# ACT issues the loads of the first modulation's weights on its own queue

## The chip, the cores and the metric

The kernel runs on one core of a Trainium2 chip. The metric is the device time of one execution in microseconds (us); shown are the median of several executions and one profiled execution with its trace.

## The reference, cut to what matters

Two transformer layers (a PixArt-like one with adaptive layer norm from a condition, then one with rotary embeddings) run over 32 sequences of 128 tokens with 256 channels, 16 heads of 16 channels, and 1024 hidden channels. The part at issue is the very first thing that layer 0 computes:

```python
mod = jax.nn.silu(t_emb) @ ada_w + ada_b        # t_emb (32, 256), ada_w (256, 1536)
shift_sa, scale_sa, gate_sa, shift_ff, scale_ff, gate_ff = jnp.split(mod, 6, axis=-1)
xm1 = _ln(x) * (1 + scale_sa) + shift_sa
qkv = (xm1 @ qkv_w + qkv_b).reshape(Bx, Nx, 3, H, HD)
```

Only `shift_sa` and `scale_sa`, the first 512 of the 1536 columns of `ada_w`, are needed before the first product with `qkv_w`. The rest of `ada_w` gives the gates and the modulation before the MLP.

## The kernel before, in words

The 32 sequences are worked through in 8 groups of 4, twice (once for each layer), and each group passes a fixed schedule of steps. One group's self-attention, cross-attention and MLP are laid over those of its neighbours. Five instruction streams (TensorE, ScalarE = ACT, VectorE = DVE, GpSimd = POOL, SyncE = SP) walk the same list of steps, `STEPS`, and meet at semaphores. Each stream's order is fixed by the code, so an instruction that waits holds back all that is behind it on its engine.

All transfers are issued by SP (lines 423 to 540), each with one `dma_start`, in this order: the condition `cond` (L427), four tiles of `x` (L429), seven small constants (L439), two transfers for the first 512 columns of `ada_w` (L441, 256 KB each, to `xs` and `side`, whose memory is free then), and then the weights of layer 0: `qkv_w` (768 KB, to `k_t`), `q_w` and `kv_w` (256 and 512 KB, to `probs_t`), the context (512 KB), `fc1_w` (1024 KB), the rest of `ada_w` (L530, 512 KB each), and more. None of these first issues waits for anything.

Every weight is split in two parts so that its products with rounded operands keep full precision. ACT makes the high part `w_hi` (L1049, a cast), DVE the low part `w_lo` (L1291, a subtraction). The first steps on each engine are:

- ACT: `Exp` of the condition (L1044, with its table load), wait for the constants, then `w_hi` of `qkv_w` when that has landed (`split_weights(0)`), then the modulation of the normalised tiles (`modulate`, L892, L897) once `mod_now` is there.
- DVE: it fills constants, makes `silu` from ACT's `Exp` (L1263 to L1267), prepares the biases once all seven constants have landed (L1270 on), takes the statistics of two tiles of `x`, makes `w_lo` of `qkv_w` (L1291, waits for `w_hi`), and only then adds the bias to the first modulation (L1281), adds one to the scales (L1286) and copies them to `mod_now` (L1170).
- TensorE: it waits for the constants, for `ada_loaded` and for `silu`, makes the first modulation (L833, 16 matmuls with `silu`, to `score`), transposes normalised tiles (L577), and multiplies with `w_hi` and `w_lo` (L546 to L548) for the first keys and queries (`p_unit`).

In the names of the trace `xs` and `side` are the two halves of `ada_w`, and `k_t<-in_L_xcond_qkv_w` is the load of `qkv_w`.

Of the kernel before, what the change touches and what calls it, by code (L numbers as in the profile page):

```python
# [16 lines left out]
P = 128  # L17
B, N, D, H = 32, 128, 256, 16
HD = D // H
DF = 4 * D  # L20
CT = D // P
# [162 lines left out]
def build_blocks(nc, a, x_mid, gates_dram, out):  # L184
    ctx = ExitStack()
    with ctx:
# [12 lines left out]
        def sem(name):  # L199
            return ctx.enter_context(nc.semaphore(name))  # L200
# [71 lines left out]
        def gate_ff(group):  # L272
# [11 lines left out]
        ada = [xs[:].rearrange("p a b c -> p (a b c)")[:, 0:6 * D],  # L284
               side[:].rearrange("p a b c -> p (a b c)")[:, 0:6 * D]]
# [24 lines left out]
        ada_loaded = sem("ada_loaded")  # L310
# [86 lines left out]
        def layer_of(group):  # L397
            return group // NG
# [26 lines left out]
        def _(sp):  # L425
            ada_w = a["L0_xcond_ada_w"].rearrange("(t p) n -> t p n", p=P)
# [3 lines left out]
            for dst, src in (  # L430
# [6 lines left out]
                (mask_cols_u8[:], a["mask_cols"]),  # L437
            ):
                sp.dma_start(dst, src).then_inc(c_loaded, 16)  # L439
            for c in range(CT):  # L440
                sp.dma_start(ada[c][:, 0:2 * D], ada_w[c, :, 0:2 * D]).then_inc(ada_loaded, 16)  # L441

            def load_weights(layer, c, to, signal):
                for name, col, kt, width in WEIGHTS[layer][c]:
# [428 lines left out]
        def _(act):  # L873
# [71 lines left out]
            def low_keys(group, unit):  # L945
                _, s, half = unit
                act.wait_ge(keys_summed, (group - NG) * 4 + 2 * s + half + 1)
                act.activation(k_t[s][:, :, 0, half * HALF:(half + 1) * HALF],
                               rot[:, 0, :].rearrange("p (t n) -> p t n", t=CT),
                               ACT.Identity, scale=head_mask[:, 0:1], bias=one_row[:, 0:1]).then_inc(keys_low, 1)  # L950
# [56 lines left out]
            def body():  # L1007
                for t in STEPS:
# [30 lines left out]
                    for group, step in live(t):  # L1039
                        if step - ACT_UNIT in UNIT_AT[layer_of(group)]:  # L1040
                            move_unit(group, UNITS.index(UNIT_AT[layer_of(group)][step - ACT_UNIT]))

            act.wait_ge(cond_loaded, 16)
            act.activation(silu_tmp[:], cond[:], ACT.Exp, scale=-1.0).then_inc(silu_step, 1)  # L1044
            act.wait_ge(c_loaded, 16 * CONST_LOADS)
# [10 lines left out]
        def _(dve):  # L1056
# [19 lines left out]
            def high_keys_out(group, n):  # L1076
                _, s, half = UNITS[n]
                dve.wait_ge(keys_low, group * 4 + 2 * s + half + 1)
                for t in range(CT):
                    op = dve.tensor_scalar(k_t[s][:, t, 1, half * HALF:(half + 1) * HALF],  # L1080
                                           p_unit[:, t * HALF:(t + 1) * HALF], head_mask[:, 1:2],
                                           key_bias[:, 1, 2 * s + t:2 * s + t + 1], ALU.mult, ALU.add)
                op.then_inc(keys_high, 1)
# [11 lines left out]
            def high_keys(group, unit):  # L1095
                _, s, half = unit
                dve.wait_ge(keys_summed, (group - NG) * 4 + 2 * s + half + 1)
                dve.tensor_scalar(k_t[s][:, :, 1, half * HALF:(half + 1) * HALF],
                                  rot[:, 0, :].rearrange("p (t n) -> p t n", t=CT),
                                  head_mask[:, 1:2], one_row[:, 1:2], ALU.mult, ALU.add).then_inc(keys_high, 1)  # L1100
# [391 lines left out]
```

## Time and profile before

| | |
|---|---|
| median of 3 executions | 1671.42 us (1670.57 to 1672.57) |
| profiled execution, its own time | 1671.03 us |
| its span, first to last instruction | 1669.2 us |
| TensorE matmul busy | 1501.2 us, 90% of the span |
| VectorE busy | 1096.9 us, 66% |
| ScalarE busy | 943.5 us, 57% |
| GpSimd busy | 719.1 us, 43% |
| mean granted TensorE clock | 0.972 |

The time lies 1.83 us above the span. Everything that the change touches happens in the first 20 us, before TensorE has its first large product.

### The profile page before, as it was taken

What the parts mean: (1) busy time and instruction counts of PE and PEld (TensorE: products, weight loads), DVE (VectorE), ACT (ScalarE), POOL (GpSimd) and SP (SyncE); (2) the same over time, 40 slices, a digit from 0 to 9 for tenths busy, and PEclk for the clock granted to TensorE, in tenths of its full rate; (3) what the DMA queues carried; (4) which work ended last, traced back from release to release, by engine and by line L of the source; (5) the groups of instructions that cost most, each with busy time, mean ns of one, the idle gap of its engine ahead of it and who ended that gap; (6) DMA issues with size and microseconds to landing.
All of it is one profiled execution on the core that took longest, in us unless ns stands there. A gap on an engine that the chain in (4) does not pass through costs nothing.

```text
span 1669.2 us, 44764 instructions
## 1 busy us (share of the span) xinstructions
PE 1501.2 (90%) x17760; PEld 1305.8 (78%) x17760; DVE 1096.9 (66%) x2373; ACT 943.5 (57%) x1722; POOL 719.1 (43%) x982
## 2 busy tenths in 40 slices
PE   4979999999999999999998989989899898989987
PEld 3868878787887878788786787878788787887866
DVE  4556766666766666667776766766767666676654
ACT  3456565556656565666645645556565555645543
POOL 3133424334242433335646445464554636455411
PEclk9899999999999999999998989999999999999988
DMA  6110100101010010100112000000000000000000
GB/s 211 47 47 10 45 16 15 52 13 55 10 46 15 15 53 13 55 27 27 33 45 65 11 17 15 14 27 11 17 15 14 26 12 17 18 24 2 2 14 14
DMA packets 34251, 49.39 MB, mean 30 GB/s; under 512 B 3488, under 2 KB 24928, under 8 KB 34048
## 3 DMA queue, kind: packets, MB, share of 16 engines
q1 hardware_dynamic: 34048, 46.54, 9.0%
q8 instruction: 145, 2.38, 0.6%
q14 instruction: 58, 0.48, 0.1%
HBM read 38.07 MB, written 8.45 MB: 28 GB/s over the span
## 4 chain that ended last, share of the span: by engine, by line
PE 67%; DVE 15%; issue 8%; ACT 8%; POOL 1%; DMA 0%; SPq 0%; DVEq 0%; ACTq 0%; POOLq 0%
PE score_t L670 8%; PE score L652 7%; PE p_unit L546 6%; PE p_unit L739 5%; PE p_mix L712 5%; PE p_unit L548 5%; PE p_unit L547 5%; DVE neg_max L1108 3%; PE p_out L548 3%; PE p_out L547 3%; PE p_out L546 3%; PE p_out L701 2%; PE p_mix L577 2%; PE score_t L546 2%; PE score_t L548 2%
## 5 line engine op out<-in xcount | busy, mean ns | idle before, releaser
L1108 DVE TENSOR_REDUCE neg_max<-score 128x8 f32<-128x1024 f32 x224 | 273.9, 1223 | 150.0 <-PE score L652 141.3
L652 PE MATMUL score<-k_t,q_t 32*128 32x256 f32 x1792 | 264.7, 413 | 54.1 <-DVE q_less L1118 28.7
L670 PE MATMUL score_t<-q_less,k_t 32*128 32x128 f32 x3584 | 273.4, 293 | 11.5 <-ACT probs_t L970 6.2
L670 PEld LDWEIGHTS score_t<-q_less,k_t 32*128 32x128 f32 x3584 | 229.8, 195 | 23.3 <-issue 14.9
L652 PEld LDWEIGHTS score<-k_t,q_t 32*128 32x128 f32 x1792 | 167.7, 194 | 94.8 <-issue 38.0
L972 ACT ACTIVATE probs_t<-score_t 128x1024 f32<-128x1024 f32 x168 | 172.0, 1024 | 113.4 <-PE score_t L670 100.7
L892 ACT ACTIVATE xt<-p_mix,mod_now 128x128 f32<-128x128 f32 x384 | 154.3, 454 | 94.3 <-PE p_mix L577 66.5
L1311 POOL TENSOR_TENSOR xt_lo<-xt,xt_hi 128x256 fp32r<-128x256 f32 x128 | 94.6, 739 | 243.1 <-ACT xt_hi L897 242.2
L739 PE MATMUL p_unit<-w_out,heads_t 128*128 128x256 f32 x512 | 144.9, 406 | 18.8 <-ACT q_t L936 8.2
L1156 DVE TENSOR_TENSOR hid_lo<-hid,hid_hi 128x256 fp32r<-128x256 f32 x256 | 145.2, 567 | 8.8
L546 PE MATMUL p_out<-w_hi,hid_lo 128*128 128x256 f32 x512 | 147.4, 288 | 0.8 <-issue 0.8
L1154 DVE CAST hid_hi<-hid 128x256 fp32r<-128x256 f32 x256 | 96.7, 378 | 73.5 <-ACT hid L957 73.4
L548 PE MATMUL p_out<-w_hi,hid_hi 128*128 128x256 f32 x512 | 144.5, 282 | 0.0
L547 PE MATMUL p_out<-w_lo,hid_hi 128*128 128x256 f32 x512 | 144.2, 282 | 0.0
L712 PE MATMUL p_mix<-probs_t,v_pad 128*32 128x128 f32 x4096 | 140.1, 278 | 0.0
L1118 DVE SCALAR_TENSOR_TENSOR q_less<-p_out,one_row,q_t 128x256 f32<-128x256 f32 x256 | 111.3, 477 | 33.8 <-PE p_out L701 33.8
L546 PE MATMUL p_unit<-xt_hi,w_lo 128*128 128x256 f32 x384 | 120.4, 314 | 11.7 <-DVE k_t L1080 7.7
L957 ACT ACTIVATE hid<-score_t,bias_cols 128x256 f32<-128x256 f32 x128 | 59.0, 475 | 117.6 <-PE score_t L548 106.6
L739 PEld LDWEIGHTS p_unit<-w_out,heads_t 128*128 128x128 f32 x512 | 87.2, 190 | 48.5 <-issue 27.3
L712 PEld LDWEIGHTS p_mix<-probs_t,v_pad 128*32 128x32 f32 x4096 | 105.2, 110 | 21.9 <-issue 21.7
L957 ACT ACTIVATE hid<-score,bias_cols 128x256 f32<-128x256 f32 x128 | 60.8, 475 | 99.7 <-PE score L548 55.6
L1304 POOL TENSOR_TENSOR rstd<-var_eps,minus_half 128x1 f32<-128x1 f32 x192 | 109.2, 569 | 15.0
(158 smaller groups left out, 4264.1 us busy)
## 6 DMA issues: line engine op xcount, KB each, us to landing
ctxt<-in_ctxT SPq DMA_DIRECT2D x16, 512.0 KB, 3.8
side<-gates SPq DMA_DIRECT2D x15, 512.0 KB, 5.5
x_new<-in_x SPq DMA_DIRECT2D x32, 128.0 KB, 2.0
x_mid<-xs SPq DMA_DIRECT2D x8, 512.0 KB, 3.4
x_new<-x_mid SPq DMA_DIRECT2D x32, 128.0 KB, 2.0
out<-xs SPq DMA_DIRECT2D x8, 512.0 KB, 2.9
k_t<-in_L_f_wT SPq DMA_DIRECT2D x2, 1024.0 KB, 5.7
probs_t<-in_L_xcond_fc_w SPq DMA_DIRECT2D x1, 1024.0 KB, 11.2
```

The lines of the kernel that those rows point to most:

```text
L546: pe.matmul(dst, lhs[1], rhs[0], start=first, stop=False, skip_group_check=shared)
L547: pe.matmul(dst, lhs[0], rhs[1], start=False, stop=False, skip_group_check=shared)
L548: return pe.matmul(dst, lhs[0], rhs[0], start=False, stop=last, skip_group_check=shared)
L652: mm = pe.matmul(score_banks(b, h)[:, r % 2, t * 2 * N:(t + 1) * 2 * N].rearrange("p (e n) -> p e n", e=2), q_t[s][rows(r), t, tokens], k_ ...
L670: mm = pe.matmul(turned_banks(b, h)[:, r % 2, x * N:(x + 1) * N], k_t[s][rows(r), t, e, tokens], q_less[rows(r), j % 2, t, e, :], start=Tr ...
L712: mm = pe.matmul(p_mix[rows(r), x * N:(x + 1) * N], v_pad[s][:, b, at:at + 32], probs_t[j % 2][:, r, x, :], start=True, stop=True, tile_po ...
L739: mm = pe.matmul(p_unit[:, 0:D], heads_t[:, t, :], w_out[:, s, t, :], start=(t == 0), stop=(t == CT - 1))
L892: op = act.activation(xt[:, k, c, :], p_mix[:, c * P:(c + 1) * P], ACT.Identity, scale=mod_now[k][:, c, b:b + 1], bias=mod_now[k][:, 2 + c ...
L957: act.activation(hid[:, u % 2, :], up_ring[u % 4][:, 0:HALF], ACT.Gelu, bias=bias_cols[:, m:m + 1])\
L972: op = act.activation(dst, src, ACT.Exp)
L1108: dve.tensor_reduce(by_half[:, 2 * h:2 * h + 2, :, :, 0], score_banks(b, h)[:].rearrange("p r (t e n) -> p r t e n", t=CT, e=2), AX.X, ALU ...
L1156: dve.tensor_tensor(hid_lo[:, u % HID_SLOTS, :], hid[:, u % 2, :], hid_hi[:, u % HID_SLOTS, :].bitcast(F32), ALU.subtract).then_inc(hid_lo ...
```

## The change

The two `dma_start` for the first 512 columns of `ada_w` leave SP's stream, where they stood ahead of `qkv_w`, and become the first two instructions of ACT's stream, on ACT's own queue. The transfers themselves, their destinations and their semaphore are the same.

```diff
                 (mask_cols_u8[:], a["mask_cols"]),
             ):
                 sp.dma_start(dst, src).then_inc(c_loaded, 16)
-            for c in range(CT):
-                sp.dma_start(ada[c][:, 0:2 * D], ada_w[c, :, 0:2 * D]).then_inc(ada_loaded, 16)
...
+            ada_w = a["L0_xcond_ada_w"].rearrange("(t p) n -> t p n", p=P)
+            for c in range(CT):
+                act.dma_start(ada[c][:, 0:2 * D], ada_w[c, :, 0:2 * D]).then_inc(ada_loaded, 16)
             act.wait_ge(cond_loaded, 16)
             act.activation(silu_tmp[:], cond[:], ACT.Exp, scale=-1.0).then_inc(silu_step, 1)
             act.wait_ge(c_loaded, 16 * CONST_LOADS)
```

SP's stream at the place of the two loads, before:

```order
L439 DMA bias_v<-in_bias_v 128x4
L439 DMA mask_cols_u<-in_mask_cols 128x32
L441 DMA xs<-in_L_xcond_ada_w 128x512
L441 DMA side<-in_L_xcond_ada_w 128x512
L447 DMA k_t<-in_L_xcond_qkv_w 128x2x768
L447 DMA probs_t<-in_L_xcond_q_w 128x2x256
```

and in the changed kernel:

```order
L439 DMA bias_v<-in_bias_v 128x4
L439 DMA mask_cols_u<-in_mask_cols 128x32
L445 DMA k_t<-in_L_xcond_qkv_w 128x2x768
L445 DMA probs_t<-in_L_xcond_q_w 128x2x256
L445 DMA probs_t<-in_L_xcond_kv_w 128x2x512
```

The load of `qkv_w` and everything after it on SP moved up by two places. ACT's stream from its first instruction, before:

```order
L872 UNCONDITIONAL_BRANCH
L1044 ACT_TABLE_LOAD
L1044 ACTIVATE silu_tmp<-cond 128x64
L1049 CAST w_hi<-k_t 128x1536
L892 ACTIVATE xt<-p_mix,mod_now 128x128 x2
```

and in the changed kernel:

```order
L870 UNCONDITIONAL_BRANCH
L1043 DMA xs<-in_L_xcond_ada_w 128x512
L1043 DMA side<-in_L_xcond_ada_w 128x512
L1045 ACT_TABLE_LOAD
L1045 ACTIVATE silu_tmp<-cond 128x64
L1050 CAST w_hi<-k_t 128x1536
L890 ACTIVATE xt<-p_mix,mod_now 128x128 x2
```

The two loads stand ahead of the table load and of the `Exp`; TensorE, VectorE and GpSimd keep their instructions and their order.

## Rows read from the trace of the kernel before

**Rows 1.** The profile's page: shares of the chain that ended last, by engine.
```profile
PE 67%; DVE 15%; issue 8%; ACT 8%; POOL 1%; DMA 0%; SPq 0%; DVEq 0%; ACTq 0%; POOLq 0%
```

**Rows 2.** The chain in order of time, first 25 us: start us, length us, what.
```profile
0.73 0.43 SPq L427
...
6.00 0.43 SPq L439
6.47 0.43 SPq L441
6.94 0.43 SPq L441
7.42 7.29 DMA k_t<-in_L_xcond_qkv_w
14.79 1.48 ACT w_hi L1049
16.29 1.76 DVE w_lo L1291
18.05 0.21 DVE mod L1281
...
23.75 0.81 ACT xt L892 x2
```

**Rows 3.** Waits of the first 45 us: engine, line <- what, us in total, times, longest.
```profile
ACT w_hi L1049 <- DMA k_t<-in_L_xcond_qkv_w: 12.0, 1, 12.0
PE score L833 <- DMA side<-in_L_xcond_ada_w: 10.1, 1, 10.1
```

**Rows 4.** DMA issues of the first 40 us: size of each, us from issue to landing.
```profile
k_t<-in_L_xcond_qkv_w SPq DMA_DIRECT2D x1, 768.0 KB, 7.3
xs<-in_L_xcond_ada_w SPq DMA_DIRECT2D x1, 256.0 KB, 2.9
side<-in_L_xcond_ada_w SPq DMA_DIRECT2D x1, 256.0 KB, 3.1
side<-in_L_xcond_ada_w SPq DMA_DIRECT2D x1, 512.0 KB, 11.9
```

**Rows 5.** DMA issues of the whole span: layer 1's weights of the same size.
```profile
k_t<-in_L_qkv_wT SPq DMA_DIRECT2D x1, 768.0 KB, 4.5
```

**Rows 6.** Windows of 1 us; the last three columns: granted clock, DMA share, GB/s.
```profile
5.00:6.00 1.00, 0.00 (x0) 0.00 (x0) 0.20 (x1) 0.00 (x0) 0.00 (x0) 1.00 0.27 40
6.00:7.00 1.00, 0.00 (x0) 0.00 (x0) 0.00 (x0) 0.00 (x0) 0.00 (x0) 1.00 0.20 15
7.00:8.00 1.00, 0.00 (x0) 0.00 (x0) 0.26 (x2) 0.00 (x0) 0.00 (x0) 1.00 0.47 49
8.00:9.00 1.00, 0.00 (x0) 0.00 (x0) 1.00 (x5) 0.00 (x0) 0.00 (x0) 1.00 0.86 307
...
14.00:15.00 1.00, 0.20 (x1) 0.00 (x0) 0.00 (x0) 0.21 (x1) 0.00 (x0) 1.00 0.99 374
```

**Rows 7.** Timeline of ACT and DVE: start us, us, engine, line, operation [idle before].
```profile
0.73 1.28 ACT L1044 ACT_TABLE_LOAD   x1 [0.73 <-PEq L1483]
2.52 0.26 ACT L1044 ACTIVATE silu_tmp<-cond 128x64 f32<-128x64 f32 x1 [0.51 <-DMA cond<-in_condT]
...
4.18 0.17 DVE L1263 TENSOR_SCALAR silu_tmp<-silu_tmp 128x64 f32<-128x64 f32 x1
4.97 0.23 DVE L1267 TENSOR_TENSOR silu<-cond,silu_tmp 128x64 f32<-128x64 f32 x1
7.74 0.17 DVE L1270 TENSOR_SCALAR bias_cols<-bias_cols 128x4 f32<-128x4 f32 x1 [2.54 <-DMA mask_cols_u<-in_mask_cols]
11.27 0.18 DVE L1066 BATCH_NORM_AGGREGATE mean_var<-stats 128x2 f32<-128x6 f32 x1
```

**Rows 8.** Timeline of TensorE: start us, us of the group.
```profile
13.11 0.61 PE L833 MATMUL score<-silu,side 128*128 128x32 f32 x2
...
25.37 0.41 PE L547 MATMUL p_unit<-xt_lo,w_hi 128*128 128x256 f32 x1
...
30.40 0.28 PE L547 MATMUL p_unit<-xt_lo,w_hi 128*128 128x256 f32 x1
```

**Rows 9.** Windows of 4 us, as in rows 6: the clock falls below full.
```profile
40.00:44.00 4.00, 3.79 (x22) 3.07 (x22) 3.93 (x6) 0.00 (x0) 2.57 (x1) 0.76 0.97 303
44.00:48.00 4.00, 3.21 (x30) 3.00 (x30) 1.74 (x3) 1.82 (x3) 0.00 (x0) 0.50 0.52 200
48.00:52.00 4.00, 4.00 (x46) 3.75 (x45) 1.62 (x3) 1.66 (x3) 0.00 (x0) 0.89 0.01 2
```

**Rows 10.** The chain in order of time at the end of that low stretch.
```profile
44.81 0.59 PE score L652
...
48.70 0.21 PE p_unit L547
...
49.07 0.12 PE p_unit L546
```

## The prediction

> **What bounds the kernel now.** The page's chain comes first: TensorE holds 67% of it, and DMA and SP's queue round to 0% [rows 1]. So the change can only pay once, at the start. The chain in order of time shows how: it begins with SP's issues at 0.73 us, walks through them one behind the other (two slots for `ada_w` at 6.47 and 6.94), waits 7.29 us for `qkv_w`, and goes on through ACT's cast, DVE's subtraction and the modulation [rows 2]. The reader is to see that the wait for `qkv_w` ends last, and that the `ada_w` transfers matter only because they stand ahead of it. The waits say the same from the other side: ACT stands 12.0 us for `qkv_w`, TensorE 10.1 us for `ada_w` [rows 3]. But TensorE's wait has slack: its last modulation matmul begins at 13.11 and takes 0.61 as a pair [rows 8], so `score` is full at 13.7, and DVE takes it only at about 18.0, when `w_lo` is done [rows 2]. That is 4.3 us of slack.
>
> **What goes.** SP loses two issues ahead of `qkv_w`. The slots begin at 6.47 and 6.94 and `qkv_w` follows at 7.42 [rows 2], so `qkv_w` is issued 0.95 us earlier, at 6.47, and so is each load behind it.
>
> Those loads also lose 2 x 256 KB, 524 thousand bytes, that were moved ahead of them. Before 8 us the DMA engines are nearly idle (40, 15 and 49 GB/s, busy share 0.27, 0.20, 0.47), and from 8 us on they are near full (307 GB/s, then 374 at 14 us) [rows 6]. So `ada_w` moves from a full stretch into an empty one.
>
> **When `qkv_w` lands.** Now at 7.42 + 7.29 = 14.71. No row shows it with nothing ahead, so I bound it.
> - Least: it takes 7.29 us as now and only the issue moves. It lands at 13.76, gain 0.95.
> - Most: it takes 4.5 us, as layer 1's weights of the same size do with little else under way [rows 5]. It lands at 10.97, gain 3.74.
> - Between: the first byte behind the issue at 6.47 still moves at the same time, now a byte of `qkv_w`. The 524 thousand bytes of `ada_w` are missing ahead of it. At some 330 GB/s, between the 307 and the 374 [rows 6], that is 1.6 us. The queue behind it is also shorter at the moment it starts, since the loads behind come one every half microsecond. From 0 to 1 us more, I take 0.2.
>
> I take 1.8 us: landing at 12.9. It is nearest to the middle case, because the loads behind `qkv_w` are as many as now, which the 4.5 us row does not have.
>
> The Trainium skill speaks against more than the least (DMA: Bandwidth & Descriptors, § Issuing engines are not separate DMA queues). It says that transfers started from several engines run on the same 16 DMA engines and interleave, and that this saves only the sequencer's issue time. By that the gain would be the two slots and the sum would end at 1670.5. The rule holds for engines that are busy throughout; the trace shows them idle where the bytes now go [rows 6], and that is why I go beyond it.
>
> **What is added, and what hides it.** ACT issues two transfers before its table load. By SP's 0.43 to 0.47 us for one [rows 2], that is 0.95 us. The table load would start at 1.68 instead of 0.73 and end at 2.96, and `Exp`, now at 2.52, would start at about 3.0 and end at 3.3 [rows 7]. DVE takes it at 4.18, after its fills. That hides it. Were the issues twice as dear (end at 4.2), it would still be hidden. And even if `silu` came 2 us later, it would not matter: it is done at 5.2, and TensorE cannot start before the constants, which DVE sees at 7.74 [rows 7]. Cost 0.
>
> On the DMA engines the `ada_w` bytes now lie beside `cond`, the four tiles of `x` and the constants. Together with `x` (4 x 128 KB) they make about a million bytes, which at the 307 GB/s of [rows 6] take 3.4 us from 2 us on. The constants are bound by their issue, the last at 6.00 [rows 2], and find the engines free. If they came late, DVE would have a cover: it has nothing to do from 11.45 to 16.29 [rows 2, 7]. After the change that cover is 16.29 - 1.8 - 11.45 = 3.0 us. Cost 0. `ada_w` must land before TensorE's 3.6 us of modulation has to start, which is 16.25 - 3.6 = 12.6 us; even the slowest landing of these first loads, 11.9 us after issue [rows 4], counted from 1.2, ends at 13.1 and would cost 0.5, and it was measured with full engines. I expect it at 5 to 6 us. Then the constants become what TensorE waits for, and its modulation runs from 7.8 to 11.4.
>
> **What is late next.** After landing, the path is `w_hi` 1.48, `w_lo` 1.76, modulation, the tiles through DVE, GpSimd, ACT and TensorE to the first product at 25.0 us. All of it is released by the step before, not by a transfer: `qkv_w` and the first `ada_w` are the large waits on transfers of the first 45 us [rows 3]. The other loads move by 0.95 us or more as well. I expect a rigid shift that goes through to the end.
>
> **Sum.** Profiled execution 1671.03 - 1.8 + 0 + 0 = 1669.2. The median shown is 0.39 above that execution, so the forecast is 1669.6 us, 0.11% faster. A measurement of this kernel tells about 0.2% (3.3 us) from no change, so this counts as the same.
>
> **Rivals.**
> 1. *Only the issue time counts* (the skill's rule, as a mechanism: `qkv_w` is slow from what is behind it, not from what is ahead, and still takes 7.29 us). For it: `qkv_w` took 7.3 us where `ada_w` ahead took 2.9 and 3.1 [rows 4]. Against it: the empty stretch [rows 6]. It gives 1671.42 - 0.95 = 1670.5.
> 2. *More than 0.2% faster.* Either `qkv_w` lands as in the most case, 1671.42 - 3.74 = 1667.7, or the clock helps. The granted clock is 0.76, 0.50 and 0.89 from 40 to 52 us [rows 9], the lower of the two levels (1.2 of 2.4 GHz) for about 7 us after a stretch where TensorE waited for DVE. A 256-column matmul takes 0.41 us at the low level and 0.28 at the high one [rows 8], and on the path each adds 0.21 or 0.12 us [rows 10]. From 44.81 to 48.91 the path is all matmuls, 4.1 us [rows 10], so at the high level it would be 4.1 x (1 - 0.12 / 0.21) = 1.8 us shorter. With the forecast's 1.8 this gives 1667.8.
> 3. *Slower.* The same clock the other way. The earlier modulation burst leaves TensorE idle sooner, and the shift puts other work under the low level. That the first products also ran low (0.41 at 25.37, 0.28 at 30.40 [rows 8]) shows that the level depends on where waits fall. Each further such stretch costs some 1.8 us. One cancels the gain. From two on the kernel is slower: 1671.42 - 1.8 + 3.6 = 1673.2. It passes 0.2% with three (1675.0). Against it: the order of work and the waits between engines are unchanged behind the first 20 us.
> 4. *The loads on ACT's queue land late.* It decides only from 12.6 us on, as worked out above, and gives more than the gain only past 14.4. I put it with rival 3.
>
> **How the numbers follow.** Forecast 0.72, rival 1 0.08, rival 2 0.15, rivals 3 and 4 0.05, of which 0.02 is past 0.2%. Faster by over 0.2%: 0.15. Within: 0.72 + 0.08 + 0.03 = 0.83. Slower: 0.02. The bounds 0.95 and 3.74 give 1670.5 and 1667.7. The three executions before span from 0.9 below to 1.2 above their median. I add 0.7 below for part of rival 2 and 1.4 above for that spread and part of rival 3: 1667.0 to 1671.9.
>
> **What would show it.** In the changed profile `qkv_w` should be issued at about 6.5 and land at about 12.9, ACT's cast should start at 13.0 and DVE's modulation at 16.2; the first large product should come 1.8 us earlier, at 23.2. ACT should issue at 0.7 and 1.2, `Exp` should start before 4.2, and TensorE's first matmul should wait for a constant at 7.8. DMA in the windows 3 to 6 us should be well above 100 GB/s. I am wrong if `qkv_w` still takes over 7 us (rival 1), if it takes under 5 (rival 2), or if the start is right and the end is not shifted; then the clock's windows behind 40 us are to be compared.

## The result, and the profile after

| | before | changed |
|---|---|---|
| median, 10 executions each | 1670.7 us (1668.69 to 1672.57) | 1666.48 us (1662.83 to 1670.85) |
| ratio | | 0.9977, 95% interval 0.9966 to 0.9987 |
| profiled execution: time, span | 1671.03, 1669.2 | 1670.85, 1669.0 |
| mean granted TensorE clock | 0.972 | 0.971 |

The changed kernel is 0.23% faster, 4.2 us between the medians (by the interval 2.2 to 5.7 us), and lies 0.5 us below the forecast range of 1667.0 to 1671.9. A second timing further down gave 1667.42 us, inside the range, and a ratio of 0.9982 (0.9969 to 0.9995). The profiled execution is the slowest of its ten; its end says little, its start a lot.

The chain in order of time of the changed kernel (columns as in [rows 2]):

```profile
6.11 0.43 SPq L439
6.58 4.54 DMA k_t<-in_L_xcond_qkv_w
11.21 1.48 ACT w_hi L1050
12.71 1.76 DVE w_lo L1292
14.47 0.21 DVE mod L1282
...
20.17 0.82 ACT xt L890 x2
```

It has the same links as [rows 2] without the two issues, and the wait for `qkv_w` shrank from 7.29 to 4.54 us. The links behind it stand 3.6 us earlier: 14.47 for 18.05, 20.17 for 23.75.

DMA issues of its first 40 us (columns as in [rows 4]):

```profile
k_t<-in_L_xcond_qkv_w SPq DMA_DIRECT2D x1, 768.0 KB, 4.5
xs<-in_L_xcond_ada_w ACTq DMA_DIRECT2D x1, 256.0 KB, 3.3
side<-in_L_xcond_ada_w ACTq DMA_DIRECT2D x1, 256.0 KB, 3.9
cond<-in_condT SPq DMA_DIRECT2D x1, 32.0 KB, 3.4
```

Windows of 1 us (columns as in [rows 6]):

```profile
3.00:4.00 1.00, 0.00 (x0) 0.00 (x0) 1.00 (x3) 0.02 (x1) 0.00 (x0) 1.00 1.07 385
...
8.00:9.00 1.00, 1.00 (x6) 1.00 (x6) 1.00 (x6) 0.00 (x0) 0.00 (x0) 1.00 0.71 237
...
12.00:13.00 1.00, 0.00 (x0) 0.00 (x0) 0.29 (x1) 0.68 (x1) 0.49 (x1) 1.00 1.05 406
```

`ada_w` is moved beside `x` at 3 to 5 us, at 385 and 357 GB/s. In the window 8 to 9 the rate is lower than before (237 against 307), from 10 us on it is higher: 383, 397 and 406 GB/s against 316, 316 and 228. The last is the row that stands out in the kernel before:

```profile
12.00:13.00 1.00, 1.00 (x7) 1.00 (x6) 0.00 (x0) 0.00 (x0) 0.35 (x1) 1.00 0.70 228
```

How many bytes were moved until `qkv_w` had landed is read from longer windows, the first two of the kernel before, the last of the changed one:

```profile
6.00:11.12 5.12, 0.99 (x5) 1.02 (x5) 2.22 (x9) 0.00 (x0) 0.74 (x2) 1.00 0.67 209
6.00:14.71 8.71, 4.07 (x18) 3.70 (x18) 2.41 (x10) 0.00 (x0) 1.49 (x4) 1.00 0.76 253
6.00:11.12 5.12, 3.23 (x16) 3.23 (x17) 2.09 (x9) 0.00 (x0) 0.75 (x2) 1.00 0.69 215
```

Up to 11.12 us, where `qkv_w` lands in the changed kernel, both kernels had moved nearly the same, 1.07 and 1.10 MB. Up to its own landing the kernel before moved 2.20 MB, though `ada_w` and `qkv_w` make only 1.31 MB of that. The other 0.89 MB belong to loads that were issued behind `qkv_w`. In the changed kernel these are 0.31 MB (1.10 less 0.79).

Timeline of ACT and TensorE in the changed kernel:

```profile
0.73 0.44 ACTq L1043 DMA_DIRECT2D xs<-in_L_xcond_ada_w  x1
1.20 0.51 ACTq L1043 DMA_DIRECT2D side<-in_L_xcond_ada_w  x1
1.74 1.28 ACT L1045 ACT_TABLE_LOAD   x1 [1.74 <-issue]
4.21 0.26 ACT L1045 ACTIVATE silu_tmp<-cond 128x64 f32<-128x64 f32 x1 [1.19 <-DMA cond<-in_condT]
```

```profile
7.89 0.64 PE L831 MATMUL score<-silu,xs 128*128 128x32 f32 x2 [7.89 <-DMA mask_cols_u<-in_mask_cols]
...
21.43 0.56 PE L544 MATMUL p_unit<-xt_hi,w_lo 128*128 128x256 f32 x1
...
26.99 0.41 PE L545 MATMUL p_unit<-xt_lo,w_hi 128*128 128x256 f32 x1
```

The two issues cost ACT 1.0 us, and `Exp` comes 1.7 us later, more than that, because `cond` now lands after 3.4 us beside the `ada_w` bytes (1.8 before). It is hidden all the same: TensorE waits for the constants, at 7.89. The first large product begins at 21.43 instead of 25.01. A unit is one set of 12 such matmuls. The last row shows a part of the gain lost again: the matmuls of the second unit take 0.41 us here and took 0.28 before [rows 8], as at the low and at the high level of the clock. This is read from the matmuls alone: the granted clock stands at 1.00 in the windows of both units, in both kernels.

### The profile page after: what moved, and what is told of

The parts are those of the page before. It is cut to its first block, busy times and chain, and to the rows that moved or that the text cites. A ratio compares the mean times of both kernels' runs of the same rounds, so it can differ in the third digit from the quotient of the medians.

```text
span 1669.0 us, 44764 instructions
## 1 busy us (share of the span) xinstructions
PE 1505.2 (90%) x17760; PEld 1308.8 (78%) x17760; DVE 1096.6 (66%) x2373; ACT 944.4 (57%) x1722; POOL 719.9 (43%) x982
## 4 chain that ended last, share of the span: by engine, by line
PE 68%; DVE 15%; issue 8%; ACT 7%; POOL 1%; SPq 0%; DMA 0%; DVEq 0%; ACTq 0%; POOLq 0%
PE score_t L668 8%; PE score L650 7%; PE p_unit L544 6%; PE p_unit L737 5%; PE p_mix L710 5%; PE p_unit L546 5%; PE p_unit L545 5%; DVE neg_max L1109 4%; PE p_out L546 3%; PE p_out L544 3%; PE p_out L545 3%; PE p_out L699 2%; PE p_mix L575 2%; PE score_t L544 2%; PE score_t L546 2%
```

## The experiments

My theory behind the result: `qkv_w` is delayed by bytes ahead of it in its ring (the queue of the engine that issues it; SP and ACT have one each), and by its issue slots, and the rest is a rigid shift (theory Q). The rivals were one slow transfer, the issue time alone, the second ring as such, and the clock. The table has one trace in each row, with what its start shows: issue of `qkv_w`, us to landing, rate in the window 12 to 13 us, start of the first product. The column MB is worked out from windows as above: what was moved from 6 us to the landing of `qkv_w`, which itself is 0.79 MB.

| kernel | place of the 512 KB | issue | to landing | GB/s | MB | first product |
|---|---|---|---|---|---|---|
| before | `ada_w` ahead, SP | 7.42 | 7.3 | 228 | 2.20 | 25.01 |
| before again (e1) | the same | 7.42 | 6.4 | 259 | 1.82 | 24.14 |
| before with transposes (e6) | the same | 7.41 | 7.8 | 161 | 2.30 | 25.48 |
| changed | ACT, early | 6.58 | 4.5 | 406 | 1.10 | 21.43 |
| changed again (e2) | the same | 6.54 | 4.3 | 399 | 1.03 | 21.17 |
| changed, timed (e12) | the same | 6.54 | 4.9 | 410 | 1.13 | 21.70 |
| changed with transposes (e7) | the same | 6.56 | 4.3 | 410 | 1.04 | 21.06 |
| e5 | ACT, early; two small loads ahead | 7.42 | 4.4 | 352 | 1.05 | 22.12 |
| e3 | SP, early | 7.40 | 4.4 | 411 | 1.17 | 22.08 |
| e4 | ACT, late (beside `qkv_w`) | 6.47 | 4.5 | 406 | 1.07 | 26.32 |
| e9 | SP, behind `qkv_w` | 6.46 | 4.2 | 372 | 1.03 | 22.95 |
| e13 | ACT early, other 2 x 256 KB ahead | 7.47 | 6.1 | 390 | 1.99 | 23.89 |
| e14 | ACT early, `kv_w` (512 KB) ahead | 7.07 | 5.6 | 397 | 1.65 | 22.97 |

**A second trace of each kernel (e1, e2).** No edit.

> The kernel before, unchanged, for a second trace. Theory Q (qkv_w is slow because of the ada_w bytes ahead of it and gets short without them): qkv_w takes about 7.3 us from issue to landing again, landing near 14.7 us, first large product near 25.0. Rival N (the 7.3 us was one slow transfer): it takes clearly less, 6 us or under. Rival C (the gain is clock): other stretches of low granted clock than in the first trace, by which later markers differ by 1 to 2 us with an equal start.

> The changed kernel, unchanged, for a second trace. Theory Q: qkv_w takes 4.5 us again and lands near 11.1, first large product near 21.4. Rival N: it takes 6 us or more this time. Rival C: the store of the last group comes at another distance from the first large product than in the first trace of the changed kernel (some 5 us), since the low clock stretches fall elsewhere.

Measured: 6.4 us for `qkv_w` in the kernel before, 4.3 in the changed one. The two groups of traces do not overlap, so the rival of one slow transfer falls, though the 7.3 us was among the longer. The clock rival holds as scatter: from the first product to the output stores that SP issues at about 1498 us the kernel before took 1473.9 and 1468.3 us in its two traces (25.01 to 1498.87, and 24.14 to 1492.43), the changed one 1477.6 and 1472.6 us (21.43 to 1498.98, and 21.17 to 1493.73). The same instructions differ by 5 us. One piece of it can be seen. In the two traces of the changed kernel the same DVE instruction (L1067) starts at 577.58 and 576.99 us, 0.6 apart, and a later one at 608.08 and 606.17, 1.9 apart. Between them lies a window whose granted clock is 0.57 in the first trace and 1.00 in the second:

```profile
588.00:592.00 4.00, 4.00 (x37) 3.65 (x34) 2.01 (x3) 1.81 (x3) 0.73 (x1) 0.57 0.99 247
```

```profile
588.00:592.00 4.00, 3.22 (x41) 2.67 (x41) 3.14 (x6) 2.89 (x4) 0.50 (x1) 1.00 0.85 257
```

The executions themselves, one each, took 1666.05 us (e1, the kernel before) and 1667.08 us (e2, the changed one), so single executions don't show the gain.

**The place of the bytes, without ACT (e3).** The two lines stand behind the load of `cond` instead of ahead of `qkv_w`, all on SP.

```diff
             sp.dma_start(cond[:], a["condT"].rearrange("(t p) b -> p t b", p=P)).then_inc(cond_loaded, 16)
+            for c in range(CT):
+                sp.dma_start(ada[c][:, 0:2 * D], ada_w[c, :, 0:2 * D]).then_inc(ada_loaded, 16)
```

> The two ada_w loads stay on SP but directly behind the condition, ahead of x; ACT issues nothing. SP's issue of qkv_w stays at 7.4 us. Theory Q: the place of the bytes counts, not the queue: qkv_w takes about 4.5 us, lands at 11.9, and the kernel is 2.8 us faster than before (0.998). Rival S (only the issue time counts): qkv_w lands at 14.7, no gain. Rival R (the second ring on ACT is what helps): no gain either, 7 us for qkv_w.

**The issue time taken out (e5).** In the changed kernel two loads of 1 KB take the two old issue slots on SP.

```diff
                 sp.dma_start(dst, src).then_inc(c_loaded, 16)
+            for c in range(CT):
+                sp.dma_start(filler[:, c], a["head_mask"]).then_inc(filled, 16)
```

> The changed kernel, with two 1 KB loads in the old places of the ada_w loads on SP, so that qkv_w is issued at 7.5 us as before. It takes the 0.95 us of issue time out of the change and leaves the rest. Theory Q: qkv_w takes 4.5 us and lands at 12.0, 2.7 us faster than before (0.9984); the difference to the changed kernel is 0.95 us. Rival S: qkv_w takes 7.3 us, no gain. It shows whether issue slots and bytes add up.

Both have `qkv_w` issued at 7.4 as before and both need 4.4 us. First product 22.08 and 22.12, as theory Q has it, 0.7 us behind the mean of the changed kernel's three traces (21.43). Timed: 0.9992 (0.9983 to 1.0002) for e3 and 0.9989 (0.9978 to 1.0001) for e5, expected 0.9983 and 0.9984. The intervals hold the expectation but also no gain, so the times alone settle nothing here; the landing does (one trace each). The effect parts into the slots and the bytes, and needs no second ring.

**The bytes beside `qkv_w` on the other ring (e4).** ACT's two issues stand behind its wait for the constants.

```diff
             act.wait_ge(c_loaded, 16 * CONST_LOADS)
+            ada_w = a["L0_xcond_ada_w"].rearrange("(t p) n -> t p n", p=P)
+            for c in range(CT):
+                act.dma_start(ada[c][:, 0:2 * D], ada_w[c, :, 0:2 * D]).then_inc(ada_loaded, 16)
```

> The changed kernel with ACT's two issues moved behind its wait for the constants (7.7 us), so that their bytes run beside qkv_w on the other ring; SP issues qkv_w at 6.5 us as in the changed kernel. Theory Q (the empty stretch is what pays): qkv_w shares the engines with half a million bytes and takes over 5 us, about 5.7, landing near 12.2; the ada_w loads take over 4 us. Rival R (a ring of its own is what pays): qkv_w takes 4.4 us as in the changed kernel. In both TensorE starts the modulation only at 12 to 13 us, and DVE may wait for it at 16.

Here theory Q was wrong. DMA issues and TensorE of e4:

```profile
k_t<-in_L_xcond_qkv_w SPq DMA_DIRECT2D x1, 768.0 KB, 4.5
xs<-in_L_xcond_ada_w ACTq DMA_DIRECT2D x1, 256.0 KB, 6.3
side<-in_L_xcond_ada_w ACTq DMA_DIRECT2D x1, 256.0 KB, 7.2
```

```profile
15.63 0.60 PE L831 MATMUL score<-silu,xs 128*128 128x32 f32 x2 [15.63 <-DMA side<-in_L_xcond_ada_w]
```

Half a million bytes beside it cost `qkv_w` nothing; it was the late ring that went slowly. `ada_w` took 6.3 and 7.2 us instead of 3.3 and 3.9, TensorE started at 15.63, and the first product came at 26.32, later than in any other trace (one execution, 1673.77 us). In this one trace the loads on the other ring did not slow `qkv_w`, and the ring that came second paid. In the changed kernel `ada_w` landed at 4.0 and 5.1 us, so my rival 4 did not come up there; e4 shows the harm that it named, when the loads are issued late.

**The same ring, other order (e9).** The kernel before, with the two loads moved behind `qkv_w` (the two old lines are gone).

```diff
             load_weights(0, 0, stage, w_loaded)
+            for c in range(CT):
+                sp.dma_start(ada[c][:, 0:2 * D], ada_w[c, :, 0:2 * D]).then_inc(ada_loaded, 16)
```

> The kernel before, with qkv_w issued ahead of the two ada_w loads, all on SP: the same ring, the same issue slots, only their order. Theory Q2 (what is ahead in the same ring delays qkv_w, what is behind does not): qkv_w, issued at 6.5, takes 4.4 us and lands at 10.9 as in the changed kernel; DMA rates from 9 to 13 us are above 380 GB/s, without the dip below 300 that the traces of the kernel before have. The ada_w loads, behind it, land at 12 to 14 us, TensorE's modulation ends at 16 to 17, and the first product begins at 22.5 to 24. Rival (the dip belongs to ada_w bytes that are moved beside weights): the dip stays and qkv_w takes over 5.5 us.

```profile
k_t<-in_L_xcond_qkv_w SPq DMA_DIRECT2D x1, 768.0 KB, 4.2
xs<-in_L_xcond_ada_w SPq DMA_DIRECT2D x1, 256.0 KB, 4.6
side<-in_L_xcond_ada_w SPq DMA_DIRECT2D x1, 256.0 KB, 4.7
```

With nothing large ahead, what stands behind in the ring costs `qkv_w` nothing that shows. `ada_w` lands at 12.2, the modulation becomes the last to be ready, and the first product begins at 22.95. Even on one ring, exchanging the two loads gives 1.2 and 2.1 us of the start, against the two traces of the kernel before (24.14 and 25.01; one execution, 1667.04 us). The dip is gone too, though the rates stay a little under the expected 380 (362 and 372 GB/s from 11 to 13 us).

**Other bytes ahead (e13, e14).** In the changed kernel, `q_w` and the first output projection (e13), or `kv_w` (e14), are issued ahead of `qkv_w`. The edit of e14, without the new argument of `load_weights` that picks one of the two loads:

```diff
+            load_weights(0, 1, stage, w_loaded, (1,))
             load_weights(0, 0, stage, w_loaded)
-            load_weights(0, 1, stage, w_loaded)
+            load_weights(0, 1, stage, w_loaded, (0,))
```

> The changed kernel, with two other 256 KB loads (q_w and the first output projection, rows of 1 KB that lie densely) in the old places of ada_w on SP, ahead of qkv_w, which is issued at 7.5. Theory A (any half million bytes ahead in the ring cost qkv_w 2 to 3.4 us, more than their 1.6 us at full rate): qkv_w takes 6.4 to 7.8 us, and the rates from 9 to 13 us fall to some 300 GB/s. Theory L (the layout of ada_w, 2 KB pieces 6 KB apart, is what makes the rate fall): qkv_w takes 4.4 + 1.6 = 6.0 us or less, at 380 GB/s and without the dip.

> The changed kernel, with kv_w (512 KB in one load, pieces of 2 KB that lie densely) ahead of qkv_w on SP: as many bytes and pieces of the same size as ada_w, but dense and in one issue, qkv_w issued at 7.0. Theory A: qkv_w takes 6.4 to 7.8 us, minus at most the 0.5 us of the missing slot, rates near 300 GB/s. Theory L: 6.0 us or less, no dip.

```profile
k_t<-in_L_xcond_qkv_w SPq DMA_DIRECT2D x1, 768.0 KB, 6.1
```

```profile
k_t<-in_L_xcond_qkv_w SPq DMA_DIRECT2D x1, 768.0 KB, 5.6
```

The first row is e13, the second e14. Half a million dense bytes ahead cost 1.7 and 1.2 us over the 4.4, about what they take at full rate (1.6 us by the prediction's working). `ada_w` ahead cost 2.0 to 3.4 us in its three traces. The 6.1 us of e13 lie between the two expectations, 0.3 us under the shortest trace of the kernel before, so with one trace each these runs don't decide between theory A and theory L.

The rates don't decide it either. Only the window 12 to 13 us sets the two layouts apart: 390 and 397 GB/s here, 161 to 259 with `ada_w` ahead. From 8 to 12 us e13 moved 303, 311, 353 and 336 GB/s, and the kernel before 307, 344, 316 and 316. The pieces of `ada_w` are 2 KB long and lie 6 KB apart; `kv_w`'s are as long and dense. That would speak for the layout, but in e9 the same pieces, issued half a microsecond later, go with 362 to 406 GB/s.

The column MB shows the other part. The kernel before moved 0.51 to 0.99 MB beyond `ada_w` and `qkv_w` before `qkv_w` had landed, and e13 0.68. The kernels with nothing large ahead moved 0.24 to 0.38 MB beyond `qkv_w`, and e14, with one dense load ahead, 0.34. Nearly all of it is from loads issued behind `qkv_w`: in the profiled execution before, `q_w`, issued at 7.89, took 6.2 us and landed at 14.1, ahead of `qkv_w` at 14.7. So with two loads of 256 KB ahead, more of what stands behind is moved first as well. Why that is so no run here shows, and no run takes the loads behind away from the kernel before.

**The clock, evened out (e6, e7).** 38 transposes of the identity into a bank that nobody uses yet fill TensorE's idle gaps of the start, in the kernel before and in the changed one.

```diff
+            def keep_busy(n):
+                for _ in range(n):
+                    pe.transpose(p_out[:, 0:P], ident[:], ident[:])
...
                             turn_z(group, 0, b)
+                            if group == 0:
+                                keep_busy((16, 7, 7, 0)[b])
...
+                            if group == 0 and step == UNIT_STEPS[0][0]:
+                                keep_busy(8)
```

> The kernel before, plus 38 transposes of the identity into an unused bank in TensorE's idle gaps between 14 and 30 us, so that its clock is at the high level before the first product. Theory K (part of the start is the low clock level): the first product's 12 matmuls take 1.6 us instead of 2.9, the time from the first product to the last store is 1 to 3 us shorter and the runs scatter less. Rival: no change of level, the time within 0.1% of before.

> The same 38 transposes in the changed kernel. It takes the clock's level at the start out of the comparison. Theory Q with K: beside the kernel before with the same transposes it is 3.0 to 3.6 us faster, the shift of its first product. If the gain is much larger than that (over 4.5) or much smaller (under 2), something behind the first product belongs to the change.

Measured: 0.9988 (0.9977 to 0.9998) for e6 and 0.9961 (0.9947 to 0.9975) for e7. Theory K did not come true: the matmuls of the first unit still took 0.41 us in both traces, and here the granted clock itself is at the low level (0.50 in the window 22 to 23 us, in both). The second unit took 0.28 in both; of the changed kernel's three traces it did so in one, but in the kernel before it did so without transposes too. So the interval of e6, which lies just under 1, has no cause in these two units, and that of e7 overlaps those of the changed kernel. That the transposes help at all is not shown. The changed kernel with transposes is 3.4 us under the other by the medians (1665.44 and 1668.88) and 4.5 us by the ratios; the first products stand 4.4 us apart in these two traces (21.06 and 25.48). This fits a gain made at the start, but the two intervals (0.10% to 0.14% to either side) leave room for some 3 us more or less. The runs of e6 did not scatter much less (1666.83 to 1673.6).

**The changed kernel timed again (e12).**

> The changed kernel once more, timed in the same job, for the size of its gain: by the start of the first product (3.0 to 3.6 us earlier in two traces of each) 0.998 of before; a gain over 5 us or under 2 would say that something behind the start belongs to the change.

0.9982 (0.9969 to 0.9995), 1667.42 us against 1671.54 in 25 executions of the kernel before, which spread from 1666.2 to 1675.58. `qkv_w` took 4.9 us.

**Further (e8, e10, e11).** The modulation now waits on DVE behind `w_lo`. e8 makes `w_lo` one step later:

```diff
-FIRST_LO_DVE_AT = {-10: 0, -4: 1, 6: 3}
+FIRST_LO_DVE_AT = {-9: 0, -4: 1, 6: 3}
```

> The changed kernel, with DVE making w_lo one step later, behind the first modulation. In the changed kernel the modulation is full at 11.9 us and waits on DVE until 14.4 for w_lo. Theory: the tiles start 2.4 us earlier (ACT's first xt at 12.8 instead of 15.2), w_lo is done before the first product all the same, the first product begins at 19.0 instead of 21.4: 2.4 us faster than the changed kernel, 5.7 us faster than before (0.9966). Rival: the tiles wait for w_lo on DVE all the same (z of the third tile), gain under 1 us.

0.9968 (0.9957 to 0.998), 1665.88 us. The expected 5.7 us came out of the medians (5.8), but that was luck: ACT's first tile starts at 12.55 as expected, and the first product only at 20.54, 0.9 us ahead of the mean of the changed kernel and not 2.4. The start accounts for 4.0 us against the kernel before (24.58 to 20.54); the rest is inside the interval. The rival was right, by a link I had not seen. GpSimd in e8:

```profile
11.84 0.19 POOL L1302 TENSOR_TENSOR var_eps<-mean_var,eps_cols 128x1 f32<-128x1 f32 x1 [1.19 <-DVE mean_var L1067]
13.85 1.61 POOL L1302 TENSOR_TENSOR var_eps<-mean_var,eps_cols 128x1 f32<-128x1 f32 x1 [1.19 <-DVE mean_var L1067]
```

The same one-column addition takes 0.19 us, or 1.61 us when it starts while DVE makes `w_lo` (13.69 to 15.42 in this trace), and `xt_lo` waits behind it. In e10 and e11 it takes 1.61 us at the same place again. The Trainium skill states such a thing (SBUF — State Buffer, § SBUF: two separate sides): a DVE operation with two SBUF inputs and a GpSimd operation that reads SBUF share a pair of ports, and whichever comes second blocks for the whole instruction of the first. The traces agree, by these rows; no run here changes DVE's operand to prove it.

e10 joins this and the transposes:

> The modulation ahead of w_lo on DVE, and the 38 transposes, together in the changed kernel. The first gave a first product at 20.5 us (0.9 us earlier), the second a high clock level at the second unit. If they add up: 0.9 us faster than with the transposes alone, 1664.5 us, some 0.996 of before.

```profile
20.12 0.36 PE L544 MATMUL p_unit<-xt_hi,w_lo 128*128 128x256 f32 x1
20.31 0.28 PE L545 MATMUL p_unit<-xt_lo,w_hi 128*128 128x256 f32 x1
```

0.9959 (0.9945 to 0.9973), 1663.98 us, the fastest median of all, though its interval overlaps those of e7, e8 and e11. The first product begins at 20.12, and here its matmuls also take 0.28 us.

e11 moves three tiles of `x` to ACT as well, so that `qkv_w` is issued at 5.04:

> The kernel of the run with the modulation first and the transposes, with three of the four tiles of x issued by ACT behind ada_w as well. SP issues qkv_w at 5.1 us instead of 6.5; it should take 4.4 us and land at 9.5; silu is late on ACT (table load at 3.2, Exp near 5) but still ahead of the constants at 6.3. First product 1.4 us earlier, at 19.1. If instead DVE's own list (statistics of two tiles) or the tiles of x bound the start, less than 0.5 us.

```profile
k_t<-in_L_xcond_qkv_w SPq DMA_DIRECT2D x1, 768.0 KB, 6.0
mask_cols_u<-in_mask_cols SPq DMA_DIRECT2D x1, 4.0 KB, 3.0
```

0.9965 (0.9954 to 0.9975), first product at 20.04: nothing more. `qkv_w` takes 6.0 us and lands at 11.0, about as in e8 (10.8). The DMA engines are busy for shares of 0.99 and 0.72 in the windows 5 to 7 us, where the changed kernel has 0.77 and 0.19, but they move only 242 and 115 GB/s there. I read it as the empty stretch being used up; no run here tests that.

## Why the prediction was wrong

**The bound** was right. The wait for `qkv_w` ended last, the `ada_w` transfers mattered only by standing ahead, and TensorE's modulation had its slack and kept it.

**The issue** was right: 0.95 us expected, 0.84 to 0.88 measured (7.42 to 6.58, 6.54).

**The landing** is the step that failed. I took 12.9, a gain of 1.8 us, as "nearest to the middle case, because the loads behind `qkv_w` are as many as now". The changed kernel's traces have it at 11.1, 10.9 and 11.4, a gain of 2.4 to 3.9 against 13.8 and 14.7 before. With nothing large ahead the loads behind cost nothing that shows: 4.2 us in e9, with `ada_w` and all weights behind it. The row that I put as the far bound, layer 1's load with 4.5 us [rows 5], was the right one to take.

The sum for the middle case had two terms, 1.6 us for the bytes of `ada_w` and 0.2 for the queue behind. The first holds as a size: up to 11.12 us the kernel before had moved as much as the changed one (1.07 and 1.10 MB), and 0.52 MB more at the 319 GB/s of its stretch from 8 us to the landing are 1.6 us, which would put the landing at 12.8. It landed at 14.7: 0.89 MB of the loads behind were moved before it (0.51 and 0.99 in the other two traces), and only 0.31 MB in the changed kernel. The difference of 0.58 MB is 1.8 us at that rate, an estimate; it says where the time is, and not why. So the term that was mis-sized is the 0.2 us for the queue behind, for which I had no row. The rate is a small part of it: the window of 12 to 13 us with 228 GB/s, which I could have read beforehand between the 307 and the 374 that I took, is 0.1 MB short of its neighbours, some 0.3 us.

**What is added** was right in its cost, nothing, and wrong in a size: `Exp` starts at 4.21 and not at 3.0, because `cond` lands late beside `ada_w` (3.1 to 3.4 us in the traces with `ada_w` on ACT early, 1.8 in e3). DVE's first cover, its fills, was just too short: it took `Exp`'s result at 4.49 and not at 4.18. The second, the constants at 7.89, held.

**The shift** goes through in the timings, as far as they can tell. The first product is 3.1 us earlier in the mean of the kernels' own traces, two and three (24.58 and 21.43), or 3.5 with the one each with transposes (24.88 and 21.34), that is 0.19% to 0.21%. Timed: 0.23% and 0.18%. (Ten executions put the kernel before at 1670.7 us, 0.7 under the three that the forecast started from.) That the shift is rigid is not shown. The prediction asked for the windows behind 40 us where the start is right and the end isn't shifted, as in the two profiled executions. The granted clock in the four windows from 36 to 52 us is 0.88, 0.70, 1.00 and 1.00 in the changed kernel, against 1.00, 0.76, 0.50 and 0.89, so the clock of these windows does not explain the loss. But by a DVE instruction at about 160 us (160.49 and 157.92 in the kernel before; 157.57, 157.12 and 157.24 in the changed one) the mean shift has shrunk from 3.1 to 1.9 us, and behind that the stretches of low granted clock lie differently from trace to trace (e2 above). For the whole run the intervals allow 2.2 to 5.7 us and 0.8 to 5.2; how much of the start's 3.1 to 3.5 reaches the end is open.

**The rivals.** Rival 1, the issue time only, is refuted by e5: with the issue where it was, `qkv_w` still takes 4.4 us. Of rival 2 the landing half came true (10.97 forecast, 10.9 to 11.4 measured; 1667.7 forecast for the time, 1666.48 and 1667.42 measured), and with a chance of 0.15 I gave it too little. Its clock half is not seen at the start: the second unit ran slower in two of three traces, not faster. Rival 3 did not carry the day, but it is real: the profiled execution of the changed kernel lost nearly all of a gain of 3.6 us by its end. Its sentence that the level depends on where waits fall is not borne out: the second unit follows the same wait of 2.29 us for DVE in the traces of the changed kernel, and takes 0.41 us a matmul in two and 0.28 in one. The spread taken from three executions (0.9 below to 1.2 above the median) was too narrow: 25 executions of the same kernel span 9.4 us.

The rule of the Trainium skill named in the prediction (DMA: Bandwidth & Descriptors, § Issuing engines are not separate DMA queues), that issuing from another engine saves only the sequencer's time, would have given 1670.5. As a forecast it falls short: the saved issue time is 0.85 us, and the first product comes 3.1 to 3.5 us earlier. The traces do agree in that the second ring itself is not what helps: in e3, all on SP, `qkv_w` takes 4.4 us too.

## What to carry to other kernels

A load that the whole start waits for should have nothing large ahead of it in its ring; then what stood behind it cost nothing that showed here. Read the landing of an equal load elsewhere in the trace as its price. And compare the bytes moved up to its landing with its own and those ahead: what is left over was issued behind it, and here it shrank with the loads ahead gone. Moving a load to another engine's queue helps when its bytes fall into an idle stretch, and turns against the kernel when they come second to a busy ring. And where TensorE's granted clock wanders, judge the mechanism of a change of some microseconds by where the first dependent instruction starts, since the totals of equal kernels scatter by more than the gain; how much of it reaches the end only many timings tell.

## What the runs showed of the hardware that was not expected

- In e4, with loads queued on SP's ring, loads on ACT's ring got about a fifth of what was moved: their 512 KB took from 7.83 to 15.5 us (8.31 + 7.2), a stretch in which the DMA engines moved 2.8 MB (an estimate, 367 GB/s for 7.68 us). SP's 768 KB, issued 1.4 us before ACT's first, was not slowed (4.5 us; 4.3 to 4.9 in the changed kernel). It is one trace.
- With two loads of 256 KB ahead in the ring, 0.51 to 0.99 MB of later loads were moved before `qkv_w` had landed, in three traces of the kernel before and in e13 (0.68). With nothing large ahead it was 0.24 to 0.38 MB, and 0.34 with one load of 512 KB ahead (e14).
- With `ada_w` ahead (pieces of 2 KB at a pitch of 6 KB) the rate fell to 161 to 259 GB/s at 12 to 13 us in three traces of three; with dense loads ahead it did not, in one trace each (390 and 397). The cause is open.
- A GpSimd addition on one column took 1.61 us instead of 0.19 while DVE subtracted two SBUF operands, in three traces of three (e8, e10, e11).
